# Attention units on TensorE: max scores before exp scores instead of after them

## What is computed

```python
qkv = (x @ qkv_w.T + qkv_b).reshape(B, T, 3, H, dh)
q, k, v = ...
scores = jnp.einsum('bhtd,bhsd->bhts', q, k) * scale
scores = jnp.where(causal, -jnp.inf, scores)
attn = jax.nn.softmax(scores, axis=-1)
seq_out = jnp.einsum('bhts,bhsd->bhtd', attn, v)
```

## Time and profile before

| | us |
|---|---|
| median of 3 runs | 800.92 |
| lowest and highest of them | 799.39, 806.83 |
| the profiled execution's own time | 804.29 |
| its span | 802.6 |
| TensorE's mean granted clock in it | 0.956 |

### The profile page before, as it was taken

The page is one execution under the profiler, slowest core; times in us unless marked ns, Lnnn a source line. Parts: engine busy times, 40 slices in busy tenths (PEclk is TensorE's granted clock), DMA queues, the critical chain, the costliest instruction groups (busy, mean ns, idle before and its releaser), DMA issues.

```text
span 802.6 us, 12373 instructions
## 1 busy us (share of the span) xinstructions
PE 715.8 (89%) x4004; PEld 500.0 (62%) x4004; DVE 604.7 (75%) x2105; ACT 351.0 (44%) x701; POOL 424.7 (53%) x334
## 2 busy tenths in 40 slices
PE   5998989998989998989999986879999999999995
PEld 2555665665656666666666754457767677676774
DVE  2257776879998889788898776547777778787785
ACT  2314555555545556465554566632224232242311
POOL 9300899995675757686776860612405134051310
PEclk9997998999999999999999996879999999999998
DMA  8786462524334334334325253032030330303000
GB/s 282 253 269 214 141 190 95 191 87 142 124 97 145 130 94 147 120 107 152 95 74 167 83 172 113 1 106 80 0 106 1 105 100 7 106 1 105 27 27 26
DMA packets 60084, 89.87 MB, mean 112 GB/s; under 512 B 7898, under 2 KB 36980, under 8 KB 60020
## 3 DMA queue, kind: packets, MB, share of 16 engines
q1 hardware_dynamic: 60020, 89.09, 34.0%
HBM read 54.72 MB, written 33.82 MB: 110 GB/s over the span
## 4 chain that ended last, share of the span: by engine, by line
PE 51%; DVE 29%; ACT 6%; issue 5%; POOL 4%; DMA 4%; SPq 1%; ACTq 0%; DVEq 0%; POOLq 0%
PE ps L1252 15%; PE ps L375 9%; DVE ps L470 7%; PE ps L339 7%; PE ps L328 7%; PE ps L316 6%; DVE Ob L518 4%; DVE A L1386 3%; PE ps L232 2%; PE ps L1217 2%; ACT X L1238 2%; ACT Pr L413 2%; DVE Z L1272 1%; DVE HL L479 1%; PE ps L352 1%
## 5 line engine op out<-in xcount | busy, mean ns | idle before, releaser
L470 DVE CUSTOM_DVE_ANT_0 ps<-ps,mask 128x256 f32<-128x256 f32 (+3 forms) x512 | 237.2, 510 | 20.9 <-PE ps L316 20.3
L413 ACT ACTIVATE Pr<-ps 128x512 f32<-128x512 f32 (+2 forms) x384 | 190.0, 529 | 117.1 <-PE ps L328 111.3
L328 PE MATMUL ps<-Q,K 98*128 98x256 f32 (+2 forms) x512 | 174.0, 382 | 12.7 <-ACT Pr L413 9.1
L316 PE MATMUL ps<-K,Q 96*128 96x256 f32 (+2 forms) x512 | 153.9, 346 | 28.5 <-DVE nmax L470 28.0
L1252 PE MATMUL ps<-ew_hi,XT 128*128 128x512 f32 x512 | 176.3, 403 | 0.0
L614 POOL TENSOR_SCALAR_AFFINE_SELECT Pr<-Pr 128x512 f32<-128x512 f32 x128 | 90.3, 721 | 141.4 <-ACT Pr L413 138.9
L1386 DVE SCALAR_TENSOR_TENSOR A<-ps,cw,A 128x256 f32<-128x256 f32 x256 | 123.6, 483 | 47.2 <-PE ps L1252 34.5
L328 PEld LDWEIGHTS ps<-Q,K 98*128 98x128 f32 x512 | 93.8, 197 | 64.5 <-ACT Pr L413 27.2
L316 PEld LDWEIGHTS ps<-K,Q 96*128 96x128 f32 x512 | 100.4, 199 | 48.8 <-DVE nmax L470 36.2
L1252 PEld LDWEIGHTS ps<-ew_hi,XT 128*128 128x128 f32 x512 | 97.1, 190 | 21.3 <-issue 0.3
L1252 PE MATMUL ps<-ew_rest,XT 128*128 128x512 f32 x256 | 101.4, 396 | 0.0
(11 more groups left out here) (190 smaller groups left out, 1044.6 us busy)
## 6 DMA issues: line engine op xcount, KB each, us to landing
qk_scratch<-HL SPq DMA_DIRECT2D x32, 512.0 KB, 2.7
Q<-qk_scratch SPq DMA_DIRECT2D x96, 128.0 KB, 2.8
K<-qk_scratch SPq DMA_DIRECT2D x96, 128.0 KB, 2.7
Pr<-xT SPq DMA_DIRECT2D x8, 512.0 KB, 5.6
xraw<-xT SPq DMA_DIRECT2D x8, 512.0 KB, 4.2
mem_scratch<-Rl SPq DMA_DIRECT2D x16, 256.0 KB, 4.0
mv_scratch<-MV SPq DMA_DIRECT2D x32, 128.0 KB, 1.7
Wm<-mem_scratch SPq DMA_DIRECT2D x2, 2048.0 KB, 9.7
```

The lines of the kernel that those rows point to most:

```text
L316: last = nc.tensor.matmul(o, Q[0:STACK, hh, P * i:P * i + P], K[0:STACK, hh, 0:n], start=True, stop=True)
L328: last = nc.tensor.matmul(o, K[0:STACK + 2, hh, P * kt:P * kt + P], Q[0:STACK + 2, hh, T - n:T], start=True, stop=True)
L413: nc.scalar.activation(probs(g % 2, kt, heads[0], len(heads)), src, ACT.Exp, scale=SCALE).then_inc(s_exp, 1)
L470: last = nc.vector.tensor_tensor_reduce(out=scores, in0=scores, in1=mask[:, T - w:T], scale=1.0, scalar=NEG, op0=ALU.add, op1=ALU.max, acc ...
```

## The change

In `pe_batch`, in each unit, the call of `pe_max_scores` now stands ahead of that of `pe_exp_scores`. Nothing else is changed. The streams of DVE, ACT, POOL and SP are word for word the same, and PE's stream holds the same instructions with the same waits.

```diff
                 for u in range(UNITS):
-                    pe_exp_scores(pe, b, g, u)
                     on, ng, nu = ahead(g, u)
                     if not (last and on):
                         pe_max_scores(pe, b + on, ng, nu)
+                    pe_exp_scores(pe, b, g, u)
                     if u in (2, 6) and not (first and g == 0):
                         for kt in ((0, 1) if u == 2 else (2, 3)):
                             pe_values(pe, pb, pg, kt)
```

## The result

| | before | after |
|---|---|---|
| median of 20 runs, us | 802.43 | 807.36 |
| lowest to highest | 798.93 to 811.59 | 802.15 to 813.72 |
| ratio after / before (95% interval) | | 1.0062 (1.004 to 1.0084) |
| profiled execution: span, mean granted clock | 802.6, 0.956 | 808.1, 0.952 |

The change makes the kernel 0.62% slower, about 5.0 us. Forecast were 3.35 us (804.3 us against a base of 800.9), within 1% of before. The ratio is that of the means of the runs; one run of the kernel before, 811.59 us, lies over 1.5% above its fastest and is left out of it.

What follows compares the result with a forecast made beforehand. PE and DVE were taken to hold each other in turn, ACT holding PE shortly and often. The terms, 2.4 + 1.6 + 0.6 - 0.7 - 0.9 + 0.35 = +3.35 us, gave 804.3 us; range 798.5 to 809.5.

Steps and rivals of the forecast that it cites:

- Term 1: Ahead of second projection, DVE holding PE: last exp score runs behind the released max score; 10 x 0.24 = 2.4 us slower.
- Term 2: Ahead of value products, DVE holding PE: exp score runs behind released max score, not inside its wait; 7 x 0.23 = 1.6 us.
- Term 3: Ahead of second projection, ACT holding PE: exp score 0.22 us later, max score saves 0.17; 12 x 0.05 = 0.6 us slower.
- Term 4: Ahead of value products, ACT holding PE: max score saves 0.23 us, ACT's chain 0.17 later; 11 x -0.06 = -0.7 us.
- E11: Exp scores of unit 11, starting ACT's chain to the value products; claimed 0.17 us later, behind a max score.
- Term 5: Single places: max scores go ahead at two long waits, -0.9 us; first exp score waits at attention's start, +0.35 us.
- E0: Exp scores of unit 0; at the start of attention they now wait for DVE too, claimed +0.35 us.
- The gap does not grow at all where ACT holds the chain: Sign in the changed profile: output transposition to the next, unchanged under ACT, about 0.2 us longer under DVE.
- Feeding DVE first: Rival: each of DVE's 33 waits for max scores shrinks by 0.24 us, 7.9 us faster, 793.0 us; chance 0.05.
- An unmoved ACT chain: Rival: ACT takes up the delay, 799.8 us; chance 0.25 together with the case of slack beside the chain.
- The clock: Rival: longer PE waits bring three more half-clock stretches, 8.8 us slower in all, 809.7 us; chance 0.15.

Runs made afterwards that it cites:

- the two halves: Against the kernel before, the exchange made in units 11, 0, 1 and 2 only: 805.22 us; in units 7 to 10 only: 805.32 us.

## Why the prediction was right, and where a term was not

The direction, the size to 1.7 us and the class (within 1%) came out. 3.35 us lies near the lower end of the measured interval (3.2 to 6.7 us), because one term had the wrong sign. Step by step:

- **Term 1** (DVE ahead of the second projection, +2.4 us): right. The piece of 0.24 us stands in the chain, and the DVE-held group grows by 0.23 us with the exchange of units 7 to 10 and by 0.22 with that of unit 10 alone. The exchange of units 7 to 10 costs 0.36% where +3.0 us (0.37%) was expected from terms 1 and 3. The prediction speaks of ten places, one with M6' as the only released one; the chain of before has eleven with the first group (at 79.41), two of them (240.52 and 359.76) with M6' alone, which makes 0.24 us more.
- **Term 2** (DVE ahead of the value products, +1.6 us for seven places): right in the piece. In after E2 takes 0.23 us behind M10, and the DVE-held group grows by 0.24 us with the exchange ahead of the value products alone. But DVE now lets M10 go at 17 places, not seven; the ten new ones are ten of the eleven of term 4.
- **Term 3** (ACT ahead of the second projection, +0.05 us a group): right. Clean groups with this half alone take 12.68 us against 12.61, and its two parts come apart in unit 10 alone, where the gain of 0.15 to 0.20 us is measured by itself. Twelve groups by 0.05 us is too little to be seen in the time.
- **Term 4** (ACT ahead of the value products, -0.06 us a group, -0.7 us): the step that failed. The forecast said that M10 "goes under E2's wait", and that ACT's chain to that wait moves back by 0.17 us. The second held: the exponentials that begin with E11's start 0.89 us behind the start of the transposes in after (at 164.29) and 0.71 before (at 163.69). The first did not. It looked at what E2 waited for and not at what M10 would wait for one place earlier. In before M10's own release, DVE's maximum of unit 7, came just while E2 ran, so that the profile shows no wait there. DVE does that maximum behind the normalisation, 1.45 us behind the transposes. Issued first, M10 meets it: 2.25 us to the value products instead of 2.12, +0.13 us a group. Exchange of unit 2 alone, the normalisation moved, and the transposes moved all show it. Eleven groups at +0.13 make +1.4 in place of -0.7 us, and the sum becomes 3.35 + 2.1 = 5.5 us against 5.0 measured (interval 3.2 to 6.7). That sum is an estimate: the 0.13 is measured in the clean groups and carried over to the others. From one trace to the other single groups with a different clock or another way of the chain move by -1.9 to +3.3 us, so that a sum that comes out to 0.5 us is in part luck.
- **Term 5**: not shown. In the opening E0's matmul runs at 68.22 in place of 67.44 us, 0.6 us later counted from the first L359, where the term had 0.35; its follow-up through ACT's copy was not in it. The gain of 0.43 us at the wait for DMA cannot be told from the profile, since the clock differed there.
- **"The gap does not grow at all where ACT holds the chain"** was wrong for the same reason as term 4: 12.61 to 12.80 us.
- **The rivals.** Feeding DVE first did what was said, DVE's waits for max scores fell by a third, and gained nothing: the chain passes from a max score to DVE's reduction at three places before and at one after. An unmoved ACT chain is excluded by the clean groups. The clock was no part of it: its mean over the 20 runs of the changed kernel was 0.959, and 0.958 to 0.959 over 85 timed runs of the kernel before. The two profiled executions differ a little (0.952 and 0.956), but in each the clock is below full level in ten of the 31 groups, and the profiles of the two halves, at 0.948 and 0.96, belong to kernels with nearly the same median time.

## What to carry to other kernels

A wait that covers one instruction may cover a second wait that no profile shows, because it ends in time. Before an instruction is moved ahead into such a wait, look up what releases it and when that ends, not only what the wait was for. Whether the exchange of two instructions ahead of a common follower pays depends on who holds the engine at that point: under a wait for the one that now comes second the other is free (unit 10, about -0.17 us), behind a wait for the one that comes first the second is added in full (+0.24 us). And short work for a third engine belongs into a wait that is there anyway: in this kernel the output transposes in unit 9 gave more than any order of the scores that was tried.

## What was not expected of the hardware

The three clean groups agree to 0.05 us within each trace (but for the one of 12.73 us), in most traces to 0.02, while runs of the same kernel spread over 12 us. In this kernel a change of about 0.1 us in a group can be read from one profile, where 12 runs of the time hardly settle 0.3%. In the changed kernel DVE's subtraction L512 took 1.23 us in some sequences and 1.89 or 2.63 in others, with the same shape. The two of 2.63 us stand in the same two sequences before and after; what it met there was not tried.
